# Sixteen rows of the first half copied inside SBUF instead of through HBM, in a two-stage convolution and rotation kernel

## What is computed

```python
x = x + conv5x5_depthwise(gn(x), kernel(weight))   # stage 1, x is (16, 128, 64, 64) float32
x = x + einsum('hvc,bchw->bvhw', R, gn(x))         # stage 2, R is (64, 128, 128)
# gn: 32 groups of 4 channels, each normalised over (4, 64, 64) of one image
```

## Time and profile before

| | |
|---|---|
| median of 3 executions | 479.38 us (477.69 to 479.73) |
| the profiled execution's own time | 481.52 us |
| its span in the trace | 479.7 us |
| TensorE busy | 423.4 us (88%) |
| VectorE, ScalarE, GpSimd busy | 361.2, 275.8, 232.5 us |
| HBM read and written | 71.32 MB, 67.12 MB |

### The profile page before, as it was taken

How to read it: one execution, slowest core, us unless ns; L and a number is a source line. 1 busy time by engine, 2 the same in 40 slices (tenths; PEclk the granted TensorE clock), 3 DMA queues, 4 the chain that set the end, 5 groups by cost and what they waited for, 6 DMA issues and landing times.

```text
span 479.7 us, 8931 instructions
## 1 busy us (share of the span) xinstructions
PE 423.4 (88%) x3225; PEld 224.6 (47%) x3225; DVE 361.2 (75%) x734; ACT 275.8 (57%) x537; POOL 232.5 (48%) x300
## 2 busy tenths in 40 slices
PE   6989979999999999999999999519999877777772
PEld 6544435555555555555555555314444333333330
DVE  5579999999999999999899976715776444555452
ACT  2356645757666576675575675316777654556530
POOL 5446646767566675766566661014444342333310
PEclk9999999999999999999999999857999998999978
DMA  9999979999989999999999999969999999999998
GB/s 166 194 175 233 250 179 253 239 252 239 253 225 234 255 235 240 243 212 254 220 246 251 249 325 305 340 97 370 416 410 413 414 415 419 416 416 416 416 406 302
DMA packets 177587, 139.03 MB, mean 290 GB/s; under 512 B 137608, under 2 KB 139656, under 8 KB 173448
## 3 DMA queue, kind: packets, MB, share of 16 engines
q1 hardware_dynamic: 158280, 105.16, 77.2%
q10 hardware_dynamic: 19264, 33.30, 23.9%
HBM read 71.32 MB, written 67.12 MB: 289 GB/s over the span
## 4 chain that ended last, share of the span: by engine, by line
PE 64%; DMA 22%; DVE 11%; issue 1%; SPq 0%; ACT 0%; DVEq 0%
PE ps L643 51%; DMA out_dram<-area 19%; PE ps L748 9%; DVE stats L539 3%; PE ps L677 3%; DVE area L614 2%; DMA x_scratch<-area 2%; DVE stats L546 2%; DVE area L531 1%; DVE area L528 1%; DVE dev L583 1%; DMA area<-x_scratch 1%; PE ps L661 0%; PE ps L653 0%; DVE area L604 0%
## 5 line engine op out<-in xcount | busy, mean ns | idle before, releaser
L643 PE MATMUL ps<-area 64*64 64x496 f32 (+2 forms) x2560 | 280.2, 588 | 4.0 <-issue 2.6
L643 PEld LDWEIGHTS ps<-area 64*64 64x64 f32 x2560 | 142.8, 133 | 94.7 <-issue 92.8
L342 POOL TENSOR_TENSOR area<-mask,area 128x325 f32<-128x325 f32 x128 | 130.8, 1045 | 62.0 <-PE ps L643 39.6
L748 PE MATMUL ps<-area 128*128 128x512 f32 x256 | 121.2, 623 | 32.0 <-DVE area L614 21.3
L614 DVE TENSOR_TENSOR area<-ps,area 128x512 f32<-128x512 f32 x128 | 82.1, 686 | 65.5 <-DMA out_dram<-area 45.7
L461 ACT ACTIVATE area<-area,norm 128x256 f32<-128x256 f32 x157 | 80.6, 588 | 66.3 <-PE ps L748 55.7
L438 ACT ACTIVATE area<-area,affine 128x256 f32<-128x256 f32 x189 | 96.4, 588 | 34.0 <-DVE affine L561 34.0
L384 POOL TENSOR_SCALAR area<-area,norm 128x256 f32<-128x256 f32 x95 | 51.8, 558 | 122.1 <-PE ps L748 90.4
L415 ACT ACTIVATE area<-ps 64x512 f32<-64x512 f32 x128 | 75.7, 591 | 42.0 <-PE ps L643 39.5
L748 PEld LDWEIGHTS ps<-area 128*128 128x128 f32 x256 | 49.0, 199 | 93.0 <-issue 56.5
L539 DVE BATCH_NORM_STATS2 stats<-area 128x6 f32<-128x512 f32 x128 | 80.3, 689 | 5.6 <-DMA area<-in_x_dram 5.6
(11 more groups left out here) (38 smaller groups left out, 90.1 us busy)
## 6 DMA issues: line engine op xcount, KB each, us to landing
area<-in_x_dram SPq DMA_DIRECT2D x252, 128.0 KB, 4.4
x_scratch<-area ACTq DMA_DIRECT2D x62, 512.0 KB, 6.4
out_dram<-area SPq DMA_DIRECT2D x15, 2048.0 KB, 17.7
area<-x_scratch SPq DMA_DIRECT2D x28, 1024.0 KB, 14.3
area<-x_scratch SPq DMA_DIRECT2D x4, 896.0 KB
out_dram<-area SPq DMA_DIRECT2D x2, 1024.0 KB, 7.8
x_scratch<-area SPq DMA_DIRECT2D x3, 256.0 KB, 6.5
area<-in_x_dram ACTq DMA_DIRECT2D x4, 128.0 KB, 4.1
```

Of the source, the lines that this page charges most:

```text
L342: last = nc.gpsimd.tensor_tensor(taps[k % TRING][:, c * KW:(c + 1) * KW].rearrange("p d (b r) -> p d b r", r=TAPS), bass.AP(tensor=of_rows ...
L643: last = nc.tensor.matmul(ps[half, bank + c].rearrange("p (j w) -> p j w", j=J)[:, :, outs], taps[k % TRING][rows, (2 * pair + c) * KW + d ...
L748: nc.tensor.matmul(ps[:, m % 6, :], rot_t[u % TURNED][:, h], gn[n % NRING][:, h], start=True, stop=True).then_inc(rotated, 1)
```

## The change

Of each group, the first 16 partitions of the sum tile (image rows 0 to 15 of images 0 to 7) no longer go to HBM. They are copied inside SBUF by one DMA for each channel, `keep_rows`, from 16 partitions into one partition (the channel's own) of a new tile `kept`: 32 KB in 16 pieces of 2 KB. `kept` is four slots of stage 2, granules 0 to 3, which are never loaded. The other 112 partitions are stored to HBM in one transfer instead of two. These four copies for each group are issued by SP, behind the loads of the group seven later, and the tile `y` is free only when both have ended (`y_free`).

Order changes with it: granules 0 to 7 are the units 0 to 3 of the first half and then of the second. Granules 4 to 10 are loaded in two pieces, channels 0 to 63 before stage 1 ends and 64 to 127 after it. SP no longer waits for earlier stores between the last group's stores. The rotation loads are spread by the waits. VectorE does the last group's second add before the norms of an older round, TensorE picks six of the last eight norms early. To make room, seven small constants lie inside `rot_all` until it is loaded.

```diff
-EXTRA = 2
-IRING = XRING + EXTRA
-EARLY = 4
-EARLY_SLOTS = (7, 8, 4, 5, 6, 0, 1, 2, 3)
-EARLY_GROUPS = (0, 28, 31, 32)
+KEPT = 4
+KEPT_ROWS = KEPT * RH
+IRING = XRING + KEPT
+SLOT_ORDER = (7, 8, 9, 10, 4, 5, 6, 0, 1, 2, 3)
+FIRST_CHANNELS = 64
...
-        slots += [piece((RH, J, W)) for _ in range(EXTRA)]
-        tin = [slots[n] for n in EARLY_SLOTS]
+        kept = piece((KEPT_ROWS, J, W))
+        slots += [kept[:, n * RH:(n + 1) * RH] for n in range(KEPT)]
+        tin = [slots[n] for n in SLOT_ORDER]
...
         def unit_half(n):
+            if n < 2 * KEPT:
+                return n % KEPT, n // KEPT
...
+        def y_free(queue, k):
+            queue.wait_ge(x1_stored[k % YRING], 16 * (k // YRING))
+            queue.wait_ge(x1_kept[k % YRING], 16 * GC * (k // YRING))
...
+        def store(queue, k, cs):
+            dst = x1_dram[k * GC + cs.start:k * GC + cs.stop].rearrange("c n h j w -> (n h) c (j w)")
+            queue.dma_start(dst[KEPT_ROWS:P], y[k % YRING][KEPT_ROWS:P, cs].rearrange("p c j w -> p c (j w)")
                             ).then_inc(x1_stored[k % YRING], 16)
+
+        def keep_rows(queue, k, cs):
+            for c in range(cs.start, cs.stop):
+                queue.dma_start(kept[k * GC + c:k * GC + c + 1].rearrange("p h j w -> p h (j w)"),
+                                y[k % YRING][0:KEPT_ROWS, c].rearrange("p j w -> p (j w)")
+                                ).then_inc(x1_kept[k % YRING], 16)
...
-            for s in range(GROUPS + 3):
+            for s in range(GROUPS + 1):
+                if s >= 2:
+                    sp.wait_ge(x1_ready, 2 * (s - 1))
                 if group(s + XRING - 2) and s >= 1:
-                    if s >= 2:
-                        sp.wait_ge(x1_ready, 2 * (s - 1))
                     load_half(sp, s + XRING - 2, 0)
                     load_half(sp, s + XRING - 2, 1)
+                if s >= 2:
+                    keep_rows(sp, s - 2, slice(0, GC))
...
+            for pair in range(2):
+                sp.wait_ge(x1_ready, 2 * GROUPS - 1 + pair)
+                keep_rows(sp, GROUPS - 1, slice(2 * pair, 2 * pair + 2))
+                store(sp, GROUPS - 1, slice(2 * pair, 2 * pair + 2))
+            load_granule(IRING - 1, slice(0, FIRST_CHANNELS))
             groups_stored(sp, GROUPS)
-            load_part(2)
+            for n in range(KEPT, IRING):
+                load_granule(n, slice(FIRST_CHANNELS, C))
...
             for n in range(GRANULES):
-                pool.wait_ge(in_landed[n % IRING], granule_landings(n))
+                if n >= KEPT:
+                    pool.wait_ge(in_landed[n % IRING], granule_landings(n))
+                elif n == 0:
+                    rows_kept(pool)
...
                 if group(s - 1) and s < GROUPS:
-                    store(act, s - 1)
+                    act.wait_ge(x1_ready, 2 * s)
+                    store(act, s - 1, slice(0, GC))
...
+                if s == GROUPS:
+                    add(s - 1, 1)
                 if is_round(s + 1):
```

More of the change, by code:

```diff
@@ L103, in conv_rotate_kernel, with early_piece @@
         used[0] = stage_end
-        slots += [piece((RH, J, W)) for _ in range(EXTRA)]
-        tin = [slots[n] for n in EARLY_SLOTS]
+        kept = piece((KEPT_ROWS, J, W))
+        slots += [kept[:, n * RH:(n + 1) * RH] for n in range(KEPT)]
+        tin = [slots[n] for n in SLOT_ORDER]
         rot_all = sb("rot_all", [C, H, C])
[L108 to L114, removed]
+        early = rot_all[:].rearrange("c h v -> c (h v)")
+        used[0] = 0
+        def early_piece(rows, shape):
+            size = 1
+            for n in shape:
+                size *= n
+            flat = early[0:rows, used[0]:used[0] + size]
+            used[0] += size
+            names = " ".join("abcd"[:len(shape)])
+            return flat.rearrange(f"p ({names}) -> p {names}", **dict(zip("abcd", shape)))
+        line = early_piece(C, (P,))
+        own_col = early_piece(TAPS * KW, (KW,))
+        phase = early_piece(TAPS * KW, (TAPS,))
+        phases = early_piece(TAPS * KW, (BLOCKS + 2, TAPS))
+        row_pick = early_piece(TAPS * KW, (TAPS, 2, HALF))
+        col_taps = early_piece(TAPS * KW, (KW, C))
+        near = early_piece(P, (HALF + BAND,))
         mask = sb("mask", [P, BAND])
@@ L165, in conv_rotate_kernel @@
         x1_stored = [sem(f"x1_stored{n}") for n in range(YRING)]
+        x1_kept = [sem(f"x1_kept{n}") for n in range(YRING)]
         norm2_stored = sem("norm2_stored")
@@ L216, in load_half, with rows_kept @@
                                 ).then_inc(x_landed[k % XRING], 16)
[L218 to L222, removed]
-                            ).then_inc(x1_stored[k % YRING], 16)
+        def store(queue, k, cs):
+            dst = x1_dram[k * GC + cs.start:k * GC + cs.stop].rearrange("c n h j w -> (n h) c (j w)")
+            queue.dma_start(dst[KEPT_ROWS:P], y[k % YRING][KEPT_ROWS:P, cs].rearrange("p c j w -> p c (j w)")
+                            ).then_inc(x1_stored[k % YRING], 16)
+        def keep_rows(queue, k, cs):
[3 more added lines that the diff above has]
+                                ).then_inc(x1_kept[k % YRING], 16)
         def groups_stored(queue, groups):
             for k in range(YRING):
[L227 to L236, removed]
+                queue.wait_ge(x1_stored[k], 16 * groups_through(k, YRING, groups)
+                              + (16 if groups == GROUPS and k == (GROUPS - 1) % YRING else 0))
+        def rows_kept(queue):
+            for k in range(YRING):
+                queue.wait_ge(x1_kept[k], 16 * GC * groups_through(k, YRING, GROUPS))
         def tap_batches():
@@ L271, in _ @@
                     sp.dma_start(rot_all[:, rows], rota_src[:, rows]).then_inc(rot_landed, 16)
[L273 to L292, removed]
+                if s == GROUPS - 1:
+                    sp.wait_ge(norm2_stored, 32 * (LAST // NBATCH))
+                    sp.dma_start(norm2[0:LAST * GC], norm2_dram[0:LAST * GC]).then_inc(norm2_landed, 16)
+                    groups_stored(sp, FIRST_CHANNELS // GC)
+                if s - 2 - (GROUPS - XRING) in range(XRING):
+                    n = s - 2 - (GROUPS - XRING) + KEPT
+                    if s >= GROUPS - 1:
+                        load_granule(n, slice(0, FIRST_CHANNELS))
+                        if s == GROUPS - 1:
+                            for m in range(KEPT, n):
+                                load_granule(m, slice(0, FIRST_CHANNELS))
+            for pair in range(2):
[3 more added lines that the diff above has]
+            load_granule(IRING - 1, slice(0, FIRST_CHANNELS))
             groups_stored(sp, GROUPS)
-            load_part(2)
+            for n in range(KEPT, IRING):
+                load_granule(n, slice(FIRST_CHANNELS, C))
             def store_rows(n, rows):
@@ L571, in _ @@
                 if group(s - 1):
-                    add(s - 1, 1)
+                    if s < GROUPS:
+                        add(s - 1, 1)
                     dve.wait_ge(x1_ready, 2 * s)
@@ L702, in turn_rotations, with pick_norms @@
                 last.then_inc(rot_turned, 1)
-            for s in range(GROUPS + 3):
+            def pick_norms(first, end):
+                for g in range(first, end):
+                    pe.wait_ge(affine_ready, g + 5)
+                    last = nc.tensor.matmul(ps[HALF:P, 0, 0:2 * J], own_group[:, g - LAST].rearrange("p n g c -> p (n g c)"),
+                                            affine[:, g + 4, 1].rearrange("p k j -> p (k j)"), start=(g == LAST), stop=(g == GROUPS - 1))
+                last.then_inc(norm2_picked, 1)
+            for s in range(GROUPS + 3):
+                if s == GROUPS + 1:
+                    pe.wait_ge(y_ready, 4 * GROUPS)
+                    pe.wait_ge(x1_ready, 2 * GROUPS)
+                    pe.wait_ge(own_group_ready, 3)
+                    pick_norms(LAST, GROUPS - 2)
                 first, first_spread = place(s), place(s) if s >= 1 else 0
@@ L717, in _ @@
                     pe.wait_ge(own_ready, 2 * GROUPS - 1)
-                    turn_rotations(0)
-                    turn_rotations(1)
+                    for u in range(PAIR + 1):
+                        turn_rotations(u)
                 for at, d in enumerate(OFFSETS):
@@ L726, in _ @@
                         average_mean(s + 2, low if at == first else high)
[L728 to L737 removed]
+            pick_norms(GROUPS - 2, GROUPS)
+            pe.wait_ge(rot_ready, PAIR + 1)
             pe.wait_ge(gn_dve, 1)
@@ L749, in _ @@
                                      start=True, stop=True).then_inc(rotated, 1)
[L750 removed]
+                if n == 0:
+                    turn_rotations(KEPT - 1)
+                elif n in (KEPT, KEPT + 1):
+                    turn_rotations(n)
+                elif n >= 2 * KEPT and n % 4 < PAIR and u + PAIR < UNITS:
                     turn_rotations(u + PAIR)
```

54 lines of the change are left out of this document (27 added, 27 removed).

## The result

The changed kernel takes 551.64 us (median of four, 550.63 to 553.73) against 479.56 us of the kernel before. The ratio is 1.149 (95% interval 1.144 to 1.154): 72 us slower, where 31 were forecast. The time lies inside the range of 466 to 558, in its "full block" part, and direction and the main mechanism, the price of the copies, are as forecast, but the size is more than twice as large.

What follows compares the result with a forecast made beforehand. TensorE, with DMA full and loading without room, bounds stage 1; bytes at 417 GB/s bound stage 2. 481.5 + 39.6 (copies) - 4 (hand-over) - 9 + 4 (stage 2) = 512 us profiled, so 510; 8-in-10 range 466 to 558.

Steps and rivals of the forecast that it cites:

- full block: Rival for stage 1's copies: they add 3.2 to 4.9 us a group, time 540 to 581 us; chance 0.17.
- What bounds before: TensorE paces stage 1 with DMA full there too; stage 2 costs its bytes over 417 GB/s.
- The copies' price, d: What stage 1's copies add to a group's loading time: taken as +2.0 us, between 0 and +4.9.
- part (5): Wider slot ring, granule order, extra turned unit, one store issue less on ScalarE, constants in `rot_all`: nothing.
- The lower bound of 0: In stage 1, SP's stall of 3.7 us a group could hold four copy issues of 0.38 us, adding 0.
- The cushions: Stage 1 slack taken off the copies' 48 us: SP's waits 5.4 us, plus 3 between VectorE and TensorE.
- The hand-over: Between the stages: last copies and stores issue without the wait, remaining loads start about 8 us after the last add: -4.
- Stage 2's bytes: Stage 2 moves 3.6 MiB less at 417 GB/s, -9 us; against it, halves going to 64 partitions, +4.
- The bound of +9.6: Stage 2's halves to 64 partitions at 199 GB/s: 18.4 us instead of 8.8; +4 was taken.
- Hidden copies: Rival for stage 1: SP's stall swallows the copies, engines reach them at different times; 470 us, chance 0.29.
- The port rule: Four neighbouring partitions share one 27.2 GB/s port: stage 1's copies add 4.2 us a group, giving 565 us.
- The signs to look for: Stage 1 loads over 10 us a group, about 190 GB/s, TensorE gaps, last add near 347 us; first normalisation 7 to 9 later.

Runs made afterwards that it cites:

- taking the destination away: The changed kernel with each group's four copies, still on SP's queue, spread over 16 partitions each instead of one: 517.98 us.
- taking the queue away: The changed kernel with each group's four copies issued on ScalarE's queue, behind its store, instead of SP's: 524.82 us.
- tiny transfers: The kernel before with extra transfers of 16 four-byte pieces for each group on SP's queue: 536.66 us with four, 507.84 us with two.

## Why the prediction came out as it did

**What bounds before, and that loading has no room: right.** Everything that held up SP or the engines came out at the end.

**The copies' price, d = +2.0 us a group: near in size** (11.17 - 9.03 = 2.14), for a reason that was half of the true one, and by some luck. The 2.14 is the net of the copies and of the store that was joined. Without copies a group's loading takes 8.56 us, so the copies add at least 2.6 and the joined store, which part (5) of the prediction put at nothing, takes off at least 0.48 (9.03 - 8.55, the kernel before with one store). I priced the destination by the four-partition pieces and let the issues hide in SP's stall. Both cost: taking the destination away leaves 1.2 us above the kernel before, taking the queue away 1.3. The lower bound of 0, that SP's stall could swallow four issues at 0.38 us, was the error here. The issue of a copy took at least 0.58 us, and the stall swallows nothing: with tiny transfers it stayed at about 3 us a group, and each further issue came on top with 0.55 us.

**The cushions, 8.4 us: wrong, the step that failed first.** Stage 1 grew by 57.6 us, not by 24 x 2.0 - 8.4. The last load was issued 53.0 us later (318.7 against 265.8), which is 24 x 2.2 with nothing taken off. Of SP's 5.4 us of waits, 2.8 were one wait at 65 to 68 us, before the loads of group 10, where the copies cost more than on average all the same (the loading of groups 7 to 10 went from 36.4 to 46.1 us, 2.4 each). The other 2.6 lay among the groups from which the 2.14 is measured, which is net of them already. The 3 us between VectorE and TensorE weren't there either: from the last load's issue to the last add it took 46.0 instead of 41.4 us. Both stretches as windows, before and then after:

```profile
265.76:307.18 41.42, 39.80 (x408) 22.71 (x403) 31.35 (x69) 25.11 (x49) 15.01 (x17) 1.00 1.02 303
```

```profile
318.74:364.77 46.03, 40.27 (x396) 22.09 (x391) 30.90 (x68) 24.08 (x47) 14.96 (x17) 0.96 0.92 220
```

TensorE was busy 40.3 us against 39.8, so its lower clock (0.96) made little of the 4.6 us. The rest is idle time: VectorE waits once more for a load of x, 5.6 us, in that stretch.

**The hand-over, -4 us: wrong in sign.** I saw that the last stores no longer wait, but counted only 0.5 MB of loads ahead of them. Five more halves stand there, issued between 363.0 and 366.1 us, since SP is late itself and reaches them only as stage 1 ends. Without them the hand-over is 12.4 us. The kernel without the copies keeps the halves, but its SP is on time with them (issued from 292.1 to 300.6 us, the last add at 307.0), and its hand-over is 7.2 us, inside the 7 to 9 that were forecast. So it was the lateness that put the halves in the way.

**Stage 2's bytes, -9 + 4: the +4 was undersized.** The bound of +9.6 was near the truth: loads to 64 partitions moved 210 GB/s, and 3.3 of the 3.8 MB were lost again (7.9 us at 417 GB/s).

**The sizes of the errors.** From the sum of 512.1 us to the profiled execution's 552.4 it is 40.3 us: 18.0 in stage 1 (57.6 instead of 39.6), 15.6 in the hand-over (+11.6 instead of -4) and 6.7 in stage 2 (+1.7 instead of -5).

**The rivals.** *Hidden copies* was wrong as a forecast, yet copies of these bytes can be free: on ScalarE's queue and to 16 partitions they are (476.7 us). In no kernel did SP's stall hide them, as this rival had it. *Full block* (540 to 581 us) held the time, but through hand-over, cushions and stage 2, with d at 2.14 and not above 3.2. The port rule of the Trainium skill (SBUF — State Buffer, on the port swizzle), by the prediction's estimate 4.8 us for 131 KB in four neighbouring partitions, gave 565 us. Its sum came nearer than mine by chance: the loading that it implies, +4.2 us, isn't what was measured (2.14), and taking the issues off SP's queue took 0.85 of that with the destination unchanged.

**The signs to look for.** The loads' pace above 10 us, 182 GB/s at a share over 1, measures that wait for DMA, and a TensorE with gaps all came. The last add at 347 and the short hand-over did not.

## What to carry to other kernels

On a queue that is already issuing all the time, count transfers before bytes: here each further one on SP's queue cost 0.55 us of a group's loading with 64 bytes and 0.39 with 32 KB to 16 partitions. Joining the two stores of a group into one gained 1.4%. An average issue longer than the median isn't room for more issues: SP's stall of 3 us a group stayed when others were added. A transfer into one partition, or loads into half of the partitions, should be priced as held engines and not by their bytes. When stage 1 gets late, whatever stands in program order at its end gets late with it, so the transfers that the next stage waits for belong in front of the prefetches on the same queue.

## What the runs showed of the hardware that I had not expected

The issue of a tiny transfer on SP's queue took 995 ns in the median where it stood behind loads of 128 KB, longer than the loads' own 636, at a DMA share of 0.73. Minimum times were alike (589 and 595 ns). Most of the long ones followed ScalarE's stores, in the kernel before too; why a store on another queue delays SP's issues, no run here shows. The issue time isn't lost for loads when ScalarE issues, but then ScalarE's own work waits. Copies by GpSimd into one partition (10.94 us) were hardly better than by SP (11.17), though SP's queue was free of them, and worse than by ScalarE (10.32); why GpSimd's are dearer than ScalarE's wasn't tried further.
